# Gathering added attention probabilities by accumulating transfers, so that TensorE sums them once a unit

## The reference

```python
x = x + attention(layernorm(x))          # 16 heads of 32, rotary positions, causal
x = x + ffn(layernorm(x))                # base matrix, plus 8 low-rank experts, top 2 gated

scores = einsum('bhqd,bhkd->bhqk', q, k) / sqrt(dk)
scores = where(causal, scores, -inf)
attn   = softmax(scores, axis=-1)
ctx    = einsum('bhqk,bhkd->bhqd', attn, v)
```

## Time and profile before

| | |
|---|---|
| median of 3 runs | 1641.5 us (1640.37 to 1641.56) |
| profiled execution | 1642.28 us |
| its span, first to last instruction | 1640.6 us |
| mean granted TensorE clock | 0.986 |
| busy: PE, DVE, POOL, ACT | 98%, 70%, 52%, 47% |

### The profile page before, as it was taken

How to read it: one execution, slowest core, us unless ns; L and a number is a source line. 1 busy time by engine, 2 the same in 40 slices (tenths; PEclk the granted TensorE clock), 3 DMA queues, 4 the chain that set the end, 5 groups by cost and what they waited for, 6 DMA issues and landing times. The chain is left out here.

```text
span 1640.6 us, 25660 instructions
## 1 busy us (share of the span) xinstructions
PE 1603.8 (98%) x9536; PEld 990.9 (60%) x9536; DVE 1145.0 (70%) x2273; ACT 763.1 (47%) x1539; POOL 845.8 (52%) x539
## 2 busy tenths in 40 slices
PE   6999999899999999999999999999999997999999
PEld 5888888555555555555555545555555445777776
DVE  6666665687777777777777767777777666666664
ACT  3222222145565656556556556655566573223221
POOL 2323234346667677767767677777767612112111
PEclk9999999689999999999999999999999999999999
DMA  5555784751134125116107107106103013222321
GB/s 198 194 199 193 224 282 154 199 123 33 28 81 101 28 53 129 28 29 147 28 21 161 28 7 174 27 8 155 33 23 110 8 33 104 78 77 77 122 84 52
DMA packets 112326, 157.06 MB, mean 96 GB/s; under 512 B 11600, under 2 KB 44880, under 8 KB 112208
## 3 DMA queue, kind: packets, MB, share of 16 engines
q1 hardware_dynamic: 102368, 136.10, 30.3%
q10 hardware_dynamic: 9840, 19.40, 3.3%
HBM read 96.23 MB, written 58.72 MB: 94 GB/s over the span
## 5 line engine op out<-in xcount | busy, mean ns | idle before, releaser
L882 ACT ACTIVATE a_probs<-a_st 128x512 f32<-128x512 f32 (+2 forms) x1244 | 579.2, 536 | 409.3 <-PE a_st L799 403.4
L749 POOL TENSOR_TENSOR a_pair<-a_probs 128x1024 f32<-128x1024 f32 (+2 forms) x300 | 576.6, 1943 | 194.0 <-ACT a_probs L882 189.0
L904 DVE TENSOR_REDUCE a_part<-a_mx 128x1 f32<-128x512 f32 (+2 forms) x864 | 551.0, 681 | 168.2 <-PE a_mx L783 130.2
L783 PE MATMUL a_mx<-a_k_stack,a_q_stack 96*128 96x512 f32 (+3 forms) x768 | 286.6, 398 | 1.2 <-DVE a_part L907 0.6
L799 PE MATMUL a_st<-a_q_stack,a_k_stack 98*128 98x512 f32 (+3 forms) x732 | 255.6, 368 | 0.0
L783 PEld LDWEIGHTS a_mx<-a_k_stack,a_q_stack 96*128 96x128 f32 x768 | 139.4, 189 | 173.0 <-DVE a_part L904 80.8
L907 DVE CUSTOM_DVE_ANT_0 a_mx<-a_mx,a_mask 128x384 f32<-128x384 f32 (+1 forms) x256 | 158.8, 631 | 79.8 <-PE a_mx L783 79.8
L270 POOL TENSOR_TENSOR p_rot<-p_mul 128x1024 f32<-128x1024 f32 x32 | 89.8, 2809 | 197.6 <-DVE p_mul L514 197.6
L783 PE MATMUL a_mx<-a_k_first,a_q_stack 96*128 96x512 f32 (+3 forms) x384 | 161.9, 445 | 3.2 <-DMA a_q_stack<-qk_scratch 2.4
L799 PEld LDWEIGHTS a_st<-a_q_stack,a_k_stack 98*128 98x128 f32 x732 | 138.1, 190 | 33.8 <-ACT a_probs L882 17.0
L733 POOL TENSOR_SCALAR_AFFINE_SELECT a_probs<-a_probs 128x512 f32<-128x512 f32 x128 | 83.1, 653 | 138.4 <-ACT a_probs L882 129.1
(11 more groups left out here) (176 smaller groups left out, 2048.8 us busy)
## 6 DMA issues: line engine op xcount, KB each, us to landing
a_q_stack<-qk_scratch SPq DMA_DIRECT2D x72, 256.0 KB, 5.0
a_k_stack<-qk_scratch SPq DMA_DIRECT2D x72, 256.0 KB, 8.2
qk_scratch<-p_rot_hi SPq DMA_DIRECT2D x32, 512.0 KB, 3.1
qk_scratch<-p_rot_lo SPq DMA_DIRECT2D x32, 512.0 KB, 3.9
v_scratch<-p_v_st SPq DMA_DIRECT2D x32, 256.0 KB, 7.1
ctx_scratch<-a_ctx_st SPq DMA_DIRECT2D x32, 256.0 KB, 2.4
f_ctx<-ctx_scratch SPq DMA_DIRECT2D x8, 1024.0 KB, 8.8
f_x<-in_x SPq DMA_DIRECT2D x8, 1024.0 KB, 7.9
```

Source lines behind the costliest of these rows:

```text
L749: pool.tensor_tensor(pair[:, p % 2, h:h + 2, q0:TT], probs[:, s % RING, h:h + 2, q0:TT], probs[:, (s + 1) % RING, h:h + 2, q0:TT], ALU.add ...
L783: mm = pe.matmul(bank[:, i, :], queries[t][0:96, head, qi * P:(qi + 1) * P], keys[par][c][0:96, head, 0:width], start=(i == 0), stop=not m ...
L882: act.activation(probs[:, s % RING, h, q0:TT], score_bank(g, HG * s + h)[:, q0:TT], ACT.Exp, scale=SCORE_SCALE).then_inc(exp_done, 1)
L904: dve.tensor_reduce(found, bank.rearrange("p (h n) -> p h n", n=width), AX.X, ALU.max).then_inc(max_done, 1)
```

## The change

The added probabilities of a unit's full pairs are gathered in one buffer. The unit's first full pair is added straight into it; each later one is added into `a_pair` as before and then added onto the gather buffer by a transfer from GpSimd's queue that accumulates (`accum_op=ALU.add`). TensorE sums the gather buffer once, with the unit's last pair; the other sums of full pairs are gone. The gather buffer is `early.x0`, which the third stage uses later; so SyncE's load of it waits for the end of group 6, and group 7 works as before. The waits on a pair's buffer follow its last user, ScalarE waits for values and additions in place of the sums, and `plan_items` weighs the pairs by what TensorE now does in them. The items for the pairs 0 to 19 in steady state were 5 5 7 8 6 6 7 8 9 8 6 5 7 9 8 8 9 7 7 5, and are then 5 7 5 8 6 8 6 8 7 8 6 8 6 8 7 8 8 7 6 8.

```diff
+UNIT_OF_PAIR = [STEPS[2 * p][0] for p in range(NPAIR)]
+GATHERED = [STEPS[2 * p][1] < UNIT_OF_PAIR[p] * SUB for p in range(NPAIR)]
+GATHER_FIRST = [GATHERED[p] and STEPS[2 * p][1] == 0 for p in range(NPAIR)]
+def gathered(g, p):
+    return g < GROUPS - 1 and GATHERED[p]
+def joins(g, p):
+    return gathered(g, p) and not GATHER_FIRST[p]
...
-    room = [width(2 * p + 2) + width(2 * p + 3) + 2 * width(2 * p) + width(2 * p + 1) + 0.7 for p in range(NPAIR)]
-    for e in LAST_PAIR:
+    room = [width(2 * p + 2) + width(2 * p + 3) + width(2 * p) + width(2 * p + 1) + 0.7 for p in range(NPAIR)]
+    for p in range(NPAIR):
+        room[p] += 0.0 if GATHERED[p] else width(2 * p)
+    for t, e in enumerate(LAST_PAIR):
+        room[e] += 1.0 if t else 0.0
         room[(e + 1) % NPAIR] -= 1.0
...
         def pairs(g, p):
-            return NPAIR * g + p + 1 + FREE
+            upto = max(0, NPAIR * g + p + 1)
+            return FREE + sum(not gathered(n // NPAIR, n % NPAIR) for n in range(upto))
+        def joined(g, p):
+            return sum(joins(n // NPAIR, n % NPAIR) for n in range(max(0, NPAIR * g + p + 1)))
+        def place_of_pair(g, p):
+            return early.x0 if gathered(g, p) and GATHER_FIRST[p] else pair[:, p % 2]
+        def wait_place_of_pair(eng, g, p):
+            n = NPAIR * g + p
+            if gathered(g, p) and GATHER_FIRST[p]:
+                t = UNIT_OF_PAIR[p] - 1 if UNIT_OF_PAIR[p] > 1 else QT - 1
+                eng.wait_ge(pair_done, pairs(g - (UNIT_OF_PAIR[p] == 1), LAST_PAIR[t]))
+                return
+            users = [m for m in range(n - 2, -1, -2) if not (gathered(m // NPAIR, m % NPAIR) and GATHER_FIRST[m % NPAIR])]
+            if not users:
+                eng.wait_ge(pair_done, FREE)
+            elif joins(users[0] // NPAIR, users[0] % NPAIR):
+                eng.wait_ge(gather_joined, 16 * joined(users[0] // NPAIR, users[0] % NPAIR))
+            else:
+                eng.wait_ge(pair_done, pairs(users[0] // NPAIR, users[0] % NPAIR))
...
+            sp.wait_ge(pair_done, pairs(GROUPS - 2, NPAIR - 1))
             sp.dma_start(early.x0[:, :, :], early.x_v[0]).then_inc(early.x_loaded[0], 16)
...
-                        pool.wait_ge(pair_done, pairs(g, p - 2))
+                        wait_place_of_pair(pool, g, p)
+                        place = place_of_pair(g, p)
                         for h in range(0, HG, 2):
                             pool.wait_ge(exp_done, exps(g, s + 1, h + 1))
-                            pool.tensor_tensor(pair[:, p % 2, h:h + 2, q0:TT], probs[:, s % RING, h:h + 2, q0:TT],
+                            pool.tensor_tensor(place[:, h:h + 2, q0:TT], probs[:, s % RING, h:h + 2, q0:TT],
                                                probs[:, (s + 1) % RING, h:h + 2, q0:TT], ALU.add).then_inc(pair_added, 1)
+                        if joins(g, p):
+                            pool.wait_ge(pair_added, 2 * (NPAIR * g + p) + 2)
+                            if joined(g, p) > 1:
+                                pool.wait_ge(gather_joined, 16 * (joined(g, p) - 1))
+                            pool.dma_start(early.x0[:, :, :], place, accum_op=ALU.add).then_inc(gather_joined, 16)
...
-                unit_first, unit_last = j == 0, p in LAST_PAIR
+                if gathered(g, p):
+                    return
+                with_gathered = t > 0 and g < GROUPS - 1
+                unit_first, unit_last = p == LAST_PAIR[t] - 1 if with_gathered else j == 0, p in LAST_PAIR
                 q0, q1 = (max(0, j + n - t * SUB) * P for n in range(2))
                 if unit_first:
                     pe.wait_ge(sum_turned, 4 * g + t + START)
+                if with_gathered and unit_last:
+                    pe.wait_ge(gather_joined, 16 * joined(g, p))
+                    for h in range(HG):
+                        pe.matmul(sum_ps[h * DK:(h + 1) * DK, :], ones[:, :], early.x0[:, h, :], start=False, stop=False,
+                                  tile_position=(0, h * DK))
...
-                    act.wait_ge(pair_done, pairs(g, p - 2))
+                    n = NPAIR * g + p - 2
+                    if n >= 0 and gathered(n // NPAIR, n % NPAIR):
+                        act.wait_ge(values_done, n + 1)
+                        act.wait_ge(pair_added, 2 * n + 2)
+                    elif n >= 0:
+                        act.wait_ge(pair_done, pairs(g, p - 2))
...
-                dve.wait_ge(pair_done, pairs(g, p - 2))
+                wait_place_of_pair(dve, g, p)
```

More of the change, by code:

```diff
@@ L595, in attend @@
         st_done, exp_done, values_done = sem("a_st_done"), sem("a_exp_done"), sem("a_values_done")
-        pair_added, pair_done = sem("a_pair_added"), sem("a_pair_done")
+        pair_added, pair_done, gather_joined = sem("a_pair_added"), sem("a_pair_done"), sem("a_gather_joined")
         av_copied, sum_turned = sem("a_av_copied"), sem("a_sum_turned")
```

## The result

| | before | after |
|---|---|---|
| median | 1641.6 us | 1670.6 us (1663.9 to 1673.8, 5 runs) |
| ratio | | 1.0156, 95% interval 1.0140 to 1.0172 |
| span of the profiled execution | 1640.6 us | 1662.2 us |

A forecast was written before the change was run, and what follows sets the result against it. TensorE, 127.99 of 128.00 us busy, bounds a group. Saving 7.74 us of sums and losing 3.1 us to late transfers gives 4.6 us a group, 32 us in seven: 1641.5 - 32.4 = 1609 us, range 1585 to 1710.

The forecast's parts named there:

- TensorE sets the time, a sum costs 0.86 us, the full gain is 54.2 us: Attention groups: TensorE alone bounds them; 9 sums fewer in each of 7 groups, 63 x 0.86 us, if nothing else is late.
- Landing 7.2 us: Accumulating 1 MB transfer, issue to landing: two reads of 2.76 us plus the store's constant 1.7 us; limits 5.6 and 11.0.
- GpSimd's issue, 1.0 us: GpSimd's own time to issue one transfer: taken as 1.0 us, between 0.37 us (SyncE's issue) and 2 us.
- The period L + 0.1: GpSimd in a run of full pairs: landing to landing, the time from issue to landing (L) plus 0.1 us.
- 4.6 us a group: Net gain in each of seven groups: 7.74 us from fewer sums less 3.1 us lost waiting in units 2 and 3.
- Break-even at L = 8.0 us: Time from a transfer's issue to its landing (L) from which the change loses; the full gain needs below 6.5 us.
- the slow transfer: Rival: landing takes over 8.0 us, as reads and write don't overlap or adding is slow; 1660 us or more; chance 0.41.
- GpSimd's issue: Rival: an issue takes 3 us, so GpSimd needs 7.9 us a pair; 3.2 us a group lost, 1664 us; chance 0.04.
- VectorE: Rival: VectorE becomes the bound, its 94.56 us now in 120 us; waits of 1 us a group, 1594 us; chance 0.04.
- Costed at nothing: Delays priced at zero, among them pair 12's additions 1.4 us later and a group's first transfer up to 3.8 us late.
- TensorE waits at the masks and sums of pairs 10 and 18 alone: Expected profile: TensorE's only waits, at pairs 10 and 18, in groups of about 123.4 us.
- the refill of the ring: ScalarE may refill a slot of the probabilities' ring only after the additions two pairs back; about 5 us of slack.

The follow-up runs named there:

- the three sizes: The changed kernel with transfers of 512 KB, 768 KB and its own 1 MB: 1588.6, 1599.7 and 1670.6 us; landings after 4.6, 5.8 and 7.2 us.
- the kernel with two gather buffers: The changed kernel with separate gather buffers for even and odd pairs in units 2 and 3, a transfer waiting for the one before the last: 1603.6 us.
- the second buffer: The changed kernel with another gather buffer for unit 2, so its first full pair needn't wait for TensorE's last sum of the unit before: 1674.2 us.

## Why the prediction was wrong, point by point

- *TensorE sets the time, a sum costs 0.86 us, the full gain is 54.2 us*: right. Without transfers a group took 120.0 us (forecast 120.3) and the kernel 1587.7 us.
- *Landing 7.2 us*: right (median 7.2). The choice held too: the bytes cost as much as two passes, on top of a constant part near the store's. That the sum is exact is in part luck: its terms were 5.5 and 1.7 us, and the three sizes give 5.2 and 2.0 us.
- *GpSimd's issue, 1.0 us*: 0.87 us, and at half size it costs nothing. The additions behind it are recorded with 5.02 us against 4.73, but their record begins 0.25 us before the issue's ends (707.10 against 706.49 + 0.86); where it begins later, as at 698.15 us in the kernel with two gather buffers, it is 4.75 us. So nothing comes on top of the 0.87 us.
- *The period L + 0.1*: mis-sized. It measured 7.64 us against 7.3, since the next issue begins 0.44 us behind the landing. By the prediction's own sums that is 4 x 0.34 us more in unit 3 and 2 x 0.34 us in unit 2, 2.0 us a group, 14 us in all. TensorE's idle time was 6.2 us a group (129 less 122.8, the mean of the six windows of groups 1 to 6) where the sum had 3.1. Of the 3.1 us too little, the period explains 2.0; the other 1.1 us are open.
- *The step that failed*: "4.6 us a group" gained took a microsecond of waiting as a microsecond. The clock's fall had no term. The mean clock of the group windows was 0.965, which is 4.5 us in 129, on top of the idle time: 120.0 + 6.2 + 4.5 = 130.7, measured 131.0. Over seven groups the clock is some 31 us and turns the sign: the idle time alone left a gain of 128.0 - 126.2 = 1.8 us a group. From the forecast gain of 32 us to the measured loss of 29 us are 61 us: the clock's 31, the idle time's 7 x 3.1 = 22, and most of the rest the 7 us by which the profiled execution was quicker than the median.
- *Break-even at L = 8.0 us*: therefore wrong. With the clock and the longer period the change loses at 7.2 us, and gains 2.6% at 5.8 us (with a quarter of the work left out).
- *The rivals*: the slow transfer was the right direction with the wrong reason, since the transfers weren't slow. GpSimd's issue, VectorE and the traffic as such were excluded by the runs.
- *Costed at nothing*: pair 12's late additions were covered; the second buffer brought no gain. The first transfer of a group falls beside the key and value loads; a landing took 10.8 us at most, and the additions of pair 5 started after 2 us of idle time that the trace puts down to nothing and that the times put down to this landing. TensorE didn't stand idle there.
- *TensorE waits at the masks and sums of pairs 10 and 18 alone*: right for 24.0 us in 14 waits for masks and 5.7 us in 6 for additions, and wrong for 12.0 us in 8 for exponentials (1.2 us of them, one wait, are there without the transfers too). The others came by the refill of the ring, which the prediction held to be covered by 5 us: four periods of 7.64 us in place of 6.2 make 5.8 us of lag by pair 17, and the exponentials of pair 19 then waited for its additions.

## What to carry to other kernels

Where each accumulating transfer waits for the landing of the one before on the same buffer, as here, the rate is one per landing, 7.64 us, though the DMA engines work on one for 5.2 us (19.8% of the span for 63); if the producer is faster than that, alternate between two buffers or break the run. No run left the wait itself out. Where TensorE is at 100%, price a wait of TensorE at its length plus 2 to 3 us for the clock (pauses of 0.6 to 0.9 us went without it, one of 1.5 us did not), and prefer losing a small certain gain (one more sum, 0.86 us) to risking such a wait once a group. A lag grows with the number of links in a row, so multiply by the longest run, not by the mean.

## What the runs showed of the hardware

An idle stretch of 3.6 us and one of 10.9 us cost nearly the same on top of themselves, 2.2 and 2.8 us in the mean, since TensorE starts at 0.50 of its clock behind either; one of 1.50 us was followed by 6.4 us at 0.50 as well. An accumulating transfer within the on-chip memory took 2.0 us and 5.2 us a MB. Issued every 6.0 us onto two buffers, such transfers landed in 7.2 and 7.5 us; they overlap only in their last and first 1.2 us or so, so this says nothing of two that move their bytes at the same time. And an issue takes 0.87 us of GpSimd, whether 512 KB or 1 MB.
